# Mamba block and top-2 MoE on one core: the urgencies and the pace of the side work set anew in every kind of batch

## The reference

```python
def _mamba_forward(hidden_states, ...):
    xz = jnp.einsum('bld,ed->bel', hidden_states, in_proj_w)
    x, z = (xz[:, :D_INNER, :], xz[:, D_INNER:, :])          # D_INNER = 1024
    x = _silu(depthwise_conv_of_4_taps(x) + conv_b)
    x_dbl = jnp.einsum('bdl,kd->blk', x, x_proj_w)           # dt_lo (32), B (16), C (16)
    delta = softplus(einsum(dt_lo, dt_proj_w) + dt_proj_b)
    def step(h, inp):                                        # 512 steps, 16 states
        h = h * jnp.exp(d_t[..., None] * A) + d_t[..., None] * B_t[:, None, :] * x_t[..., None]
        return (h, jnp.sum(h * C_t[:, None, :], axis=-1))
    ...
    y = (ys + x * D) * _silu(z)
    return jnp.einsum('bld,ed->ble', y, out_proj_w)

x = layernorm(x + mamba(x))
top_vals, top_idx = top_k(x @ gate_w.T, 2);  w = softmax(top_vals)
x = layernorm(x + sum over the two experts of w * (x @ expert_w[e].T + expert_b[e]))
```

## Time and profile before

| | |
|---|---|
| median of 3 runs | 2318.35 us (2313.05 to 2318.67) |
| the profiled execution | 2313.4 us, of which the span from the first to the last instruction 2311.6 us |
| busy | PE 89%, PEld 53%, DVE 88%, ACT 68%, POOL 80% |
| granted TensorE clock, mean | 0.934 |
| HBM | 299.37 MB read, 85.72 MB written |

### The profile page before, as it was taken

One profiled execution on the slowest core, in us unless ns is written; L12 is line 12 of the kernel. 1 busy time (PEld: TensorE's weight loads), 2 busy tenths in 40 slices (PEclk: granted clock), 3 DMA queues, 4 the chain that ended last, 5 costly groups with the idle time before them and its releaser, 6 DMA issues.

```text
span 2311.6 us, 30515 instructions
## 1 busy us (share of the span) xinstructions
PE 2057.2 (89%) x8624; PEld 1224.0 (53%) x8624; DVE 2038.8 (88%) x2314; ACT 1575.7 (68%) x2823; POOL 1847.7 (80%) x1505
## 2 busy tenths in 40 slices
PE   8896779897999989899898998999898999879898
PEld 3444455555555555555555555555555555556453
DVE  5899999999999989898998999999998999899923
ACT  5758856786577866678577875778666885656522
POOL 2959998799887989879897899879898797786503
PEclk9897879998999999899999999999999999779999
DMA  5513142368554685457763587546854577575685
GB/s 173 171 52 85 38 138 81 123 206 274 175 135 155 224 287 142 128 174 228 259 159 108 181 275 243 135 155 226 287 148 128 165 246 251 148 233 180 220 292 118
DMA packets 222086, 412.79 MB, mean 179 GB/s; under 512 B 29881, under 2 KB 36153, under 8 KB 221921
## 3 DMA queue, kind: packets, MB, share of 16 engines
q1 hardware_dynamic: 194848, 348.58, 44.2%
q0 software_dynamic: 20496, 57.16, 12.3%
q10 hardware_dynamic: 6576, 5.11, 0.9%
HBM read 299.37 MB, written 85.72 MB: 167 GB/s over the span
## 4 chain that ended last, share of the span: by engine, by line
POOL 31%; PE 28%; DVE 15%; issue 12%; ACT 7%; DMA 6%; SPq 2%; DVEq 0%; POOLq 0%; ACTq 0%
PE bank L1105 20%; POOL hst L1608 15%; DVE hst L1826 6%; PE hTp L1121 5%; POOL first_dbu L1608 4%; DVE y L1648 4%; POOL delta L1591 2%; POOL u L1594 2%; DVE hst L1834 2%; DMA zs<-sorted_tokens 2%; DVE u L1677 2%; POOL u L1557 1%; ACT dA L1482 1%; POOL sorted_tokens L1536 1%; DMA ysb<-sorted_results,place 1%
## 5 line engine op out<-in xcount | busy, mean ns | idle before, releaser
L1482 ACT ACTIVATE dA<-delta,negA 128x512 f32<-128x512 f32 (+1 forms) x1152 | 720.1, 638 | 369.0 <-DVE hst L1826 294.7
L1608 POOL TENSOR_TENSOR hst<-u,Bbc 128x512 f32<-128x512 f32 x672 | 884.8, 1417 | 30.0 <-PE hTp L1121 29.6
L1826 DVE TENSOR_TENSOR_SCAN hst<-dA,hst 128x512 f32<-128x512 f32 x672 | 788.0, 1206 | 27.2 <-ACT dA L1482 22.9
L1121 PEld LDWEIGHTS hTp<-ident,hst 128*128 128x128 f32 x4096 | 512.1, 152 | 350.1 <-issue 150.4
L1121 PE MATMUL hTp<-ident,hst 128*128 128x128 f32 x4096 | 577.8, 294 | 131.3 <-DVE hst L1826 34.0
L1648 DVE SCALAR_TENSOR_TENSOR y<-hTp,Ct,y 128x1024 f32<-128x1024 f32 x463 | 585.0, 1263 | 48.9 <-PE hTp L1121 45.3
L1608 POOL TENSOR_TENSOR first_dbu<-u,Bbc 128x512 f32<-128x512 f32 x224 | 293.4, 1390 | 15.8 <-DVE hst L1826 11.0
L1826 DVE TENSOR_TENSOR_SCAN hst<-dA,first_dbu 128x512 f32<-128x512 f32 x224 | 265.0, 1208 | 11.6 <-ACT dA L1482 6.0
L1105 PE MATMUL bank<-wslot,hidT 128*128 128x512 f32 x512 | 244.7, 613 | 19.6 <-ACT zs L1412 15.2
L1105 PE MATMUL bank<-wslot,tokT 128*128 128x512 f32 x480 | 225.9, 602 | 8.5 <-ACT ysb L1455 6.1
L1105 PE MATMUL bank<-delta,tokT 128*128 128x512 f32 x480 | 223.2, 601 | 0.7 <-ACT tokT L1425 0.7
(11 more groups left out here) (168 smaller groups left out, 2797.9 us busy)
## 6 DMA issues: line engine op xcount, KB each, us to landing
wslot<-in_w_expT SPq DMA_DIRECT2D x90, 1024.0 KB
Bbc<-b_scratch SPq DMA_DIRECT2D x113, 256.0 KB
zs<-sorted_tokens SPq DMA_DIRECT2D x105, 256.0 KB, 4.6
sorted_results<-ysb SPq DMA_DIRECT2D x105, 256.0 KB, 6.6
wslot<-in_w_inT SPq DMA_DIRECT2D x26, 1024.0 KB
y<-scaled POOLq DMA_DIRECT2D x49, 512.0 KB, 5.3
res<-in_w_expT SPq DMA_DIRECT2D x18, 1024.0 KB, 6.1
gate_scratch<-zs SPq DMA_DIRECT2D x64, 256.0 KB, 2.0
```

Source lines behind the costliest of these rows:

```text
L1121: mm = nc.tensor.transpose(hTp[q % 2][:, tok(j)], hst[n % 2][:, j, start:start + P], ident[:, :])
L1482: nc.scalar.activation(decay_of(step, halved), delta[w.odd][:, j, cols], ACT.Exp, scale=negA[:, j, n:n + 1]).then_inc(exp_done, 1)
L1608: nc.gpsimd.tensor_tensor(dbu_row(n, j), u[w.odd][:, j, :], Bbc[n % 2][:, :], ALU.mult).then_inc(dbu_done, 1)
L1826: nc.vector.tensor_tensor_scan(hst[n % 2][:, j, :], dA[j % 2][:, :], dbu_row(n, j), 0.0, ALU.mult, ALU.add).then_inc(scan_done, 1)
```

## The change

In the four kinds of batch whose list is sorted by urgency, the bonus of each group gets a new number, and so does the pace: 0.36 to 0.64 in `SEG_PRO`, 0.6 to 0.64 in `SEG_TWO`, 0.45 to 0.78 in `SEG_FULL`, 0.64 to 0.6 in `SEG_EPI`. No operation, buffer, semaphore or assumed cost changes; each engine does the same instructions in another order. The whole diff:

```diff
-SEG_PRO = Segment(by_urgency({"ZB": -95, "Z": 7, "lb": -12, "lW": 135, "px": 47, "ps": -104, "pp": 76, "sk": -47, "py": 6, "pd": 21}), 0.36, W_Z + W_X, W_Z)
-SEG_TWO = Segment(by_urgency({"py": -29, "Zb": -25, "m0": 265, "ld": -335, "o0": 167, "o1": 65, "ln": -114, "sc": -365, "mb": 157, "pd": -13, "lx": -74, "px": 177, "ps": -4, "m1": -115, "Za": 77, "m2": 120, "m3": -270, "mw": -224, "pp": -137, "sk": -196}), 0.6, W_TWO + W_O + GAP + [experts(2, LATE)], [x[0] for x in W_L])
-SEG_FULL = Segment(by_urgency({"pp": 601, "sk": -728, "L0": 544, "L1": -443, "m0": -364, "m1": 319, "Zb": 489, "py": 206, "m2": -212, "pd": -190, "mb": -113, "m3": 283, "mw": -202, "ld": 659, "o0": 214, "o1": -22, "ln": -52, "sc": -284, "lx": 49, "px": -126, "ps": -323, "Za": -835, "E0": 141, "E1": 446}), 0.45, W_FULL + W_O + GAP + [experts(2, LATE)], [x[0] for x in W_L])
-SEG_EPI = Segment(by_urgency({"L0": 754, "L1": 601, "mw": 834, "m0": -733, "ld": 50, "oe": -409, "of": -45, "ln": -901, "sc": 273, "mb": -570, "m1": -1015, "E0": 745, "E1": 329, "m2": 1528, "m3": 586, "m4": -96, "nz": 25, "ha": 608, "hd": -128, "hm": 370, "lz": 86}), 0.64,
+SEG_PRO = Segment(by_urgency({"ZB": -886, "Z": 354, "lb": -1165, "lW": -696, "px": -699, "ps": -30, "pp": -302, "sk": -497, "py": -809, "pd": -14}), 0.64, W_Z + W_X, W_Z)
+SEG_TWO = Segment(by_urgency({"py": 43, "Zb": -98, "m0": 356, "ld": -548, "o0": 101, "o1": -35, "ln": -574, "sc": -412, "mb": 1121, "pd": -222, "lx": 14, "px": -33, "ps": -7, "m1": 65, "Za": 386, "m2": -261, "m3": -143, "mw": -325, "pp": -241, "sk": -290}), 0.64, W_TWO + W_O + GAP + [experts(2, LATE)], [x[0] for x in W_L])
+SEG_FULL = Segment(by_urgency({"pp": 646, "sk": -967, "L0": 579, "L1": -460, "m0": -351, "m1": 364, "Zb": 434, "py": 120, "m2": -212, "pd": -189, "mb": -712, "m3": 94, "mw": -368, "ld": 678, "o0": 50, "o1": 93, "ln": -60, "sc": -273, "lx": -144, "px": -184, "ps": -342, "Za": -825, "E0": 235, "E1": 173}), 0.78, W_FULL + W_O + GAP + [experts(2, LATE)], [x[0] for x in W_L])
+SEG_EPI = Segment(by_urgency({"L0": 833, "L1": 654, "mw": 799, "m0": -815, "ld": 70, "oe": -139, "of": 21, "ln": -887, "sc": 279, "mb": -501, "m1": -1033, "E0": 672, "E1": 329, "m2": 1588, "m3": 578, "m4": -203, "nz": -39, "ha": 615, "hd": -128, "hm": 372, "lz": 86}), 0.6,
```

## The result

The changed kernel takes 2327.51 us in the median of 22 runs (2319.51 to 2340.75) against 2313.28 us (22 runs, 2303.25 to 2326.83) of the kernel before: a ratio of 1.0059, 95% interval 1.0047 to 1.0071, so some 14 us slower. The forecast was 2305 us and faster, with 2284 to 2326 as its range.

A forecast was written before the change was run, and what follows sets the result against it. The prediction took DVE's work plus its idle time to bound the scanned part. Its terms, 0 - 5 - 4 - 1 = -10 us, gave 2303.4 from the profiled execution or 2308 from the median; it said 2305 us, range 2284 to 2326.

The forecast's parts named there:

- the reversal at row 108: Full batches, PE: dt(5) goes ahead of moe(5); taken at -1.0 us a batch, -5 us in five.
- The chain from ACT's 1.57 us: Late in full batches: ACT waits for a store, delaying yinit copies, PE's transpose, then DVE; at most about 1.2 us a batch.
- the lower side: Full batches: later moe matmuls and transposes could delay a state part by at least 2.4 us a batch, +12 in five.
- the rest of the sum: Terms outside the full batches' reversals: pace 0, SEG_EPI 0, batch 0 -4 us, batch 1 -1 us.
- The rival for the slower side: Full batches and batch 1: dt(5) ahead of moe(5) pushes last tokens past row 127; 14 to 21 us slower, chance 0.17.
- The pace: All segments: a higher pace lets one ready DVE piece go one row earlier; costed at 0.
- SEG_EPI: Batch 7: 47 of 305 decisions contested, none reversed; cost 0, batch 7 keeps its 279.5 us.
- Batch 0: SEG_PRO: ten reversals, nine of z against x on PE, move later work ahead by up to ten rows; -4 us.
- Batch 1: SEG_TWO: about 20 of 108 contested decisions reversed, in both directions; -1 us, bounds -8 and +8.
- The frame: Scanned part: DVE's work stays the same and a new order changes only its idle time, together 152 us.
- the rival by the clock: Batch 0: steadier PE keeps the upper clock level, idle time of batches 0 and 1 goes; -27.6 us, chance 0.02.
- a sign of being wrong in its root: Full batches differing by more than 4 us each, or batch 7 by more than 2, would show small planner shifts grow.

The follow-up runs named there:

- the later edit: Last accumulating DMA of each batch issued behind row 122 instead of 123; with dt at -189, ratio 0.9974 to the kernel before, 2308.47 us.

## Why the prediction was wrong

**The step that failed** is the price of the reversal at row 108, "I take -1.0 a batch". The reversal was found, and its place too, but both halves of its price were wrong. First, the gain was argued from the wrong wait. The chain from ACT's 1.57 us to DVE's first wait of 1.60 ends before the reversal begins to act; that wait is 1.60 us in every full batch of all seventeen profiles, and ACT's is 1.50 in the changed kernel. What shrank is the second wait, and the direct gain is 0.57 us a batch (3.46 to 2.89). Second, the lower side was argued from PE's matmuls alone, and the DMAs that the moved pieces issue were put at nothing, without a reason. `moe(7)` and `xsT(10)` carry a 1 MB load and a 256 KB load on SP's queue, and moving them brought these close to the last accumulating DMA of the batch, for which DVE then waits 15.6 us in five batches. Measured: ratio 1.0056 for that one number, +13 us or 2.6 us a batch, against -5 us foretold. The term was 18 us off, and the rest of the sum, -5 us, was within 5 us: without the reversal the change measures 0.9996.

**The rival for the slower side** was right in its sign and near in its size (14 to 21 us), and near in its place, the last rows of the batch. That is luck, for its mechanism was wrong: no `moe` was pushed past row 127; one piece fewer stands there.

**The pace** was costed at 0, measured 1.0019 (0.9995 to 1.0043). Right in time; wrong was that only one piece would move: in batch 0 many pieces shifted.

**`SEG_EPI`** was said to have no reversal. It has one that I overlooked: 2 MB of Wo go ahead of `szE(2)` and `szE(3)` on SP (70 + 189 = 259 against 255 and 244, where before it was 239). It costs nothing, 1.0004. That batch 7 would be at 279.5 us within 1 us fails (282.5), but by nothing the change did: kernels with the old table had 276.4 to 283.5.

**Batch 0** was taken at -4 us and is worth -2. **Batch 1** was taken at -1 and gives nothing that can be measured (0.9991 alone).

**The frame** held in part. DVE's work is the same and idle time moved; the few reversals of `SEG_FULL` are those foretold; the granted clock of batch 0 stayed at 0.83 while its length fell by 2.9 us, so the rival by the clock found no support. But the prediction named a sign of being wrong in its root, full batches that differ by more than 4 us each, and one of them does (267.0 to 275.1 us; the other four by -1.7 to 3.4). Single full batches vary by up to 6.2 us between kernels with the same tables, so the sign proves little; what the tables show is plainer. One reversal dragged `xsT(10)` along by eight rows and turned the order of two loads, and comparing single contests in the old tables can't foretell that.

## What to carry to other kernels

Before a wait is counted as the gain of a reversal, look whether it lies behind the reversed decision; here the first of the two lay ahead of it. When a piece of work is moved in a timetable, list the transfers that it issues or releases, and look what else is in flight at their new place, above all a transfer with a reader that is due soon. The margin to check is not whether a transfer waits today, but by how much it lands before it is needed: here 5 us of landing time had become 10, and the plan, which holds no time for this DMA's landing, gave no sign of it. And when a small edit of a planner's numbers loses time, the number that does it can be found by putting single numbers back; here one unit in one of 24 carried the whole loss, and one row for one DMA took it away.

## What was not expected of the hardware

A DMA that adds 512 KB into y landed after 5.1 to 5.4 us with no 1 MB load issued within 2.8 us of it, and after 9.2 to 11.1 us with one issued 0.7 to 1.1 us ahead, in each of the five full batches of the three kernels without the later edit. Issued 0.1 to 0.2 us ahead of such a load instead, it took 6.6 to 10.3 us (three kernels).

The other accumulating DMAs of the full batches say the same, in fifteen kernels (those with all DMAs two rows earlier left aside): 154 with a 1 MB load issued at most 1.3 us ahead landed after 8.2 to 11.1 us, 294 with none in the 2.9 us ahead or the 2 us behind landed after 4.5 to 6.2; the other 77 took 4.9 to 10.3. So the slow landing is no news of the change: in the kernel before, the first and the sixth of each full batch already take 8.4 to 9.8 us, and no DVE instruction waits for them. This is a correlation over different places in the batch, not a test with the load taken away; which of the transfers in flight slows the DMA, the expert loads, the token tiles or the stores, was not separated.

The kernels with every such DMA two rows earlier lost 26 us, of which some 24 lie in five executions of a DVE instruction of 0.15 us that took 3.2 to 5.6 us, each ending within 0.04 us of the end of a run of POOL operations with no gap. In the kernel before POOL was idle when that instruction came, in batches 1 to 6. Why it is held, and why the long scans beside the same POOL operations are not, no run here shows.
